# Graph attention on one core: a gather that leaves out the edges outside a slot's block of nodes

## The chip, the core and the metric

The kernel runs on one core of a Trainium2 chip. The metric is the device time of one execution in microseconds. The core has the engines TensorE (PE), VectorE (DVE), ScalarE (ACT) and GpSimd (POOL), the queue of SyncE (SP), which issues plain DMAs, and 16 DMA engines. Gathers by a list of indices are issued from GpSimd's queue.

## What is computed

One layer of graph attention with 12,500 nodes of 128 numbers, 200,000 edges with 64 numbers each, and 4 heads of 32. The edges come sorted by destination. The reference, cut to what matters (`_layernorm` and the first `maximum` make `h`):

```python
dst = jnp.minimum((12500 * jax.random.uniform(key, (200000,)) ** 2.0).astype(jnp.int32), 99999)
_o = jnp.argsort(dst, stable=True); src = src[_o]; dst = dst[_o]
...
h = jnp.maximum(_layernorm(x, axis=-1), 0.0)
h = (h @ W_node.T).reshape(num_nodes, H, HD)
e = (edge_features @ W_edge.T).reshape(num_edges, H, HD)
att = jnp.sum(jnp.concatenate([h[src], h[tgt], e], axis=-1) * a, axis=-1)
att = jnp.where(att > 0, att, 0.2 * att)
m = jnp.maximum(jax.ops.segment_max(att, tgt, num_segments=num_nodes), 0.0)
ex = jnp.exp(att - m[tgt])
denom = segment_sum(ex, tgt) + (num_edges - deg)[:, None] * jnp.exp(-m)
h_prime = segment_sum((ex / denom[tgt])[:, :, None] * h[src], tgt)
x = x + h_prime.reshape(num_nodes, H * HD)
```

## The kernel before

The nodes form 98 blocks of 128, the edges 1563 tiles of 128. A tile's edges can have destinations in more than one block. The kernel therefore works on slots: a slot is a tile together with one block, and a tile that reaches into a second block gets a second slot with the same 128 edges. There is room for 1664 slots (NS), in 52 groups (NG) of 32 (G), and each group has two halves of 16 (GS).

The program has four stages, each of which ends with all engines waiting for each other.

Stage 1 makes the tables of slots, nearly all of it on VectorE, in a chain in which each operation waits for the one ahead (`link`). With TensorE it selects for each slot the source indices `src_i` (one column of 128 a slot), the block `block_s`, and `rel_s`, the destination counted from the start of the slot's block: 0 to 127 for an edge inside the block, negative or 128 and more for one outside. The loop over `TB` = 13 column blocks (lines 295 to 306) copies these out; behind it come `block_1h` (line 308), the indices of the edge scores and the flags of chunks, which SyncE's queue stores to memory (line 193).

Stage 2 makes the table of nodes, `node_table`: for each node its 128 projected numbers and 4 scores, 528 bytes. GpSimd only sets `acc`, the sums of all nodes, to zero here (line 432).

Stage 3 is the loop over the groups. GpSimd gathers for each slot the 128 table rows of its source indices into `gath`, which holds two groups (line 661); once a group it gathers the edge scores too (line 650). After every 16 gathers it waits until they have landed (`PACE`). SyncE's queue loads the edges' numbers, TensorE and ScalarE make the edge scores from them. VectorE adds the scores (line 866, which needs the group's gathers), forms running maxima, multiplies the rows with the weights into `vals` (line 959) and adds each slot's sums to its block in `acc` (line 996), whose number is read at run time. Each slot has a one-hot matrix `onehot_b` (line 845: is `rel_s` equal to the column's number), whose rows for edges outside the block are all zero; TensorE multiplies it with `vals` (line 726), so the outside edges add zero times what stands in their rows.

Stage 4 divides the sums, adds `x` and stores the output.

The order on each engine is the order in which the code is written: GpSimd's queue in stage 3 is 32 gathers of line 661 a group, one of line 650 ahead of the 25th, and the two waits.

Of the kernel before, what the change touches and what calls it, by code (L numbers as in the profile page):

```python
# [14 lines left out]
P = 128  # L15
N_BLOCKS = -(-N_NODES // P)
N_TILES = -(-N_EDGES // P)
TB = -(-(N_TILES + N_BLOCKS - 1) // P)
NS = TB * P
G = 32  # L20
GS = G // 2
# [7 lines left out]
HC = HD + 1  # L29
ACC = HEADS * HC  # L30
PAD_DST = 1 << 20
NODE_GROUP = 7
N_NODE_GROUPS = N_BLOCKS // NODE_GROUP
EPS = 1e-5


def gat_kernel(nc, x, src, dst, ea, w_node, w_edge, a, out):
    f32, bf16, i32 = mybir.dt.float32, mybir.dt.bfloat16, mybir.dt.int32
    ALU = mybir.AluOpType
# [9 lines left out]
    with ctx:  # L49
        def sb(name, shape, dt):  # L50
            return ctx.enter_context(nc.sbuf_tensor(name, shape, dt))
# [19 lines left out]
        src_i = sb("src_i", [P, NS], i32)  # L71
        rel_s = sb("rel_s", [P, NS], bf16)
# [37 lines left out]
        def v3(t, cols):  # L110
            return t.rearrange("p (a c) -> p a c", c=cols)
# [3 lines left out]
        def tmp(n):  # L115
            off = [0]
            for m in (NS,) * 5 + (2 * P * TB,):
                off.append(off[-1] + m)
            return acc[:, off[n]:off[n + 1]]

        t_dst, t_a, t_b, t_c, t_last = tmp(0), tmp(1), tmp(2), tmp(3), tmp(4)
        sel = tmp(5).rearrange("p (k s) -> p k s", k=TB)
        gath_flat = gath[:, :, :, :].rearrange("p a s r -> p (a s r)")
# [10 lines left out]
        i_iota = of_flat[:, 0:2 * P].bitcast(i32)  # L134
        reset = src_i[:, :].bitcast(f32)
        tile_s, tile_here = t_b, t_c
        i_firstkey, key_t = oh_flat[:, 0:NS], oh_flat[:, NS:2 * NS]

        with ExitStack() as stage:
            def ssem(name):  # L140
                return stage.enter_context(nc.semaphore(name))
# [26 lines left out]
            def tiles(n):  # L168
                return dst[n:n + NS * P].rearrange("(k q p) -> q k p", q=P, p=P)

            with nc.Block() as block:  # L171
                @block.sync
                def _(sp):
                    sp.dma_start(v3(i_dst, P), tiles(1)).then_inc(s_ints, 16)
                    sp.dma_start(v3(i_src, P), src.rearrange("(k q p) -> q k p", q=P, p=P)).then_inc(s_ints, 16)
                    sp.dma_start(v3(i_other, P), tiles(0)).then_inc(s_prev, 16)
                    sp.dma_start(wn[:, :], w_node).then_inc(s_w, 16)
                    for j in range(2):
                        sp.dma_start(we2[:, j, :], w_edge).then_inc(s_w, 16)
                    sp.wait_ge(s_amat0, 1)  # L180
                    for h in range(HEADS):
                        sp.dma_start(a_mat[h * HD:(h + 1) * HD, h:3 * HEADS:HEADS],
                                     a[h, :].rearrange("(s d) -> d s", s=3),
                                     allow_slow_non_contiguous=True).then_inc(s_a, 16)
                    sp.wait_ge(s_prev_free, 1)
                    sp.dma_start(v3(i_other, P), tiles(2)).then_inc(s_next, 16)
                    sp.wait_ge(s_chunk, 1)
                    sp.dma_start(prev_keys[1:C, :, 0:1], chunk_keys[0:C - 1, 1, :, P - 1:P], allow_slow_non_contiguous=True).then_inc(s_prevkey, 16)
                    sp.dma_start(prev_keys[0:1, 1, 0:1], chunk_keys[C - 1:C, 1, 0, P - 1:P]).then_inc(s_prevkey, 16)
                    sp.wait_ge(s_flags, 1)  # L190
                    for b in range(2):
                        w = min(C, NG - b * C)
                        sp.dma_start(flags[b * C:b * C + w, :, :], chunk_flags[0:w, b, :, :]).then_inc(s_flags_out, 16)
                    sp.wait_ge(s_flags_out, 32)
# [21 lines left out]
                def _(dve):  # L216
                    step = [0]

                    def link(ins):

                        step[0] += 1
                        ins.then_inc(s_dve, 1)
                        dve.wait_ge(s_dve, step[0])

                    V = nc.vector
# [63 lines left out]
                    for k in range(TB):  # L289
                        link(V.tensor_scalar(vals[:, 0:2, 0:P], v3(iota[:, :], P), before[:, k:k + 1], None, ALU.is_ge))  # L290
                        V.scalar_tensor_tensor(out=sel[:, k, :].rearrange("p (c s) -> p c s", s=P), in0=v3(iota[:, :], P), scalar=end[:, k:k + 1],
                                               in1=vals[:, 0:2, 0:P], op0=ALU.is_lt, op1=ALU.mult).then_inc(s_sel, 1)
                        dve.wait_ge(s_sel, k + 1)

                    for k in range(TB):
# [7 lines left out]
                                               op0=ALU.mult, op1=ALU.add).then_inc(s_selfree, 1)  # L303
                        dve.wait_ge(s_selps, 2 * k + 2)
                        V.tensor_copy(i_firstkey[:, c], bank[3][:, 0:P])
                        V.tensor_copy(tile_s[:, c], bank[3][:, P:2 * P]).then_inc(s_selfree, 1)
                    dve.wait_ge(s_selfree, 2 * TB)
                    link(V.tensor_scalar(block_1h[:, :], block_s[:, :], pcol[:, 0:1], None, ALU.is_equal))
                    link(V.tensor_scalar(block_row[:, :], block_s[0:1, :], float(N_BLOCKS), None, ALU.min))
                    link(V.scalar_tensor_tensor(out=slot_no[:, :], in0=block_s[:, :], scalar=-float(P), in1=i_firstkey,  # L310
                                                op0=ALU.mult, op1=ALU.add))
# [85 lines left out]
        with ExitStack() as stage:  # L397
# [5 lines left out]

            W = NODE_GROUP
            WP = NODE_DIM + 2 * HEADS
# [12 lines left out]
            s_split, s_ttps, s_acc0 = ssem("tgt_split"), ssem("tgt_transposed"), ssem("acc_zeroed")  # L418
# [10 lines left out]
            with nc.Block() as block:  # L429
                @block.gpsimd  # L430
                def _(pool):
                    pool.memset(acc[:, :], 0.0).then_inc(s_acc0, 1)  # L432

                @block.sync
# [135 lines left out]
        with ExitStack() as stage:  # L570
# [7 lines left out]
            s_g = [ssem(f"rows_gathered{q}") for q in range(4)]  # L578
# [24 lines left out]
            def iterations(eng, start, body, finish):  # L603
                start(Group(0))
                for n in range(NG):
                    body(Group(n), n > 0, n + 1 < NG, n + 2 < NG)
                finish(Group(NG - 1))

            with nc.Block() as block:
# [34 lines left out]
                @block.gpsimd  # L644
                def _(pool):
                    def gather_edges(g):
                        for t in (min(g.n, NTG - 1), min(g.n, NTG - 1) - 1):
                            if t >= 0:
                                pool.wait_ge(s_er[t % 2], 16 * (t // 2 + 1))
                        nc.gpsimd.indirect_dma_start(  # L650
                            out=edge_t[:, g.r, :], out_offset=None, in_=edge_rows[0:min(g.n + 1, NTG) * P, :],
                            in_offset=bass.IndirectOffsetOnAxis(ap=edge_idx[:, g.n:g.n + 1], axis=0)).then_inc(s_et[g.r], 16)

                    def body(g, prev, nxt, second):
                        for a in range(2):
                            if g.n >= 2:
                                pool.wait_ge(s["vals"], g.n * 2 + a - 3)
                            for j in range(GS):
                                if a == 1 and j == GS // 2:
                                    gather_edges(g)  # L660
                                nc.gpsimd.indirect_dma_start(  # L661
                                    out=gath[:, g.r, a * GS + j, :], out_offset=None, in_=table,
                                    in_offset=bass.IndirectOffsetOnAxis(ap=src_i[:, g.n * G + a * GS + j:g.n * G + a * GS + j + 1], axis=0)).then_inc(s_g[2 * g.r + a], 16)
                                if j % PACE == PACE - 1:
                                    pool.wait_ge(s_g[2 * g.r + a], g.use * (16 * GS) + 16 * (j + 1))

                    iterations(pool, lambda g: None, body, lambda g: None)
# [165 lines left out]
                def _(dve):  # L833
# [131 lines left out]
                    def load_blocks(g, a):  # L965
                        blocks = []
                        for part in range(GS // 8):
                            _, b = nc.values_load_multi_w_load_instructions(
                                block_row[:, ds(g.n * G + a * GS + 8 * part, 8)], engines=[mybir.EngineType.DVE], min_val=0,
                                max_val=N_BLOCKS, skip_runtime_bounds_check_because="clamped to N_BLOCKS in stage 1")  # L970
                            blocks += b
                        return blocks
# [55 lines left out]
        with ExitStack() as stage:  # L1028
# [5 lines left out]

            W = 2 * NODE_GROUP
            n_out = N_BLOCKS // W
# [70 lines left out]
```

## Time and profile before

| | |
|---|---|
| time, median of 3 runs | 2682.41 us (2681.25 to 2682.56) |
| the profiled execution | 2685.02 us, its span 2682.7 us |
| busy share of the span | PE 45%, PEld 38%, DVE 64%, ACT 22%, POOL 61% |
| stage 1, 2, 3, 4 | 0 to 150.9, to 262, to near 2633, to 2682.7 us |
| memory | 183.85 MB read, 16.31 MB written, 75 GB/s over the span |
| granted TensorE clock, mean | 0.683 |

The span is the time from the first to the last instruction of the core; what the time has beyond it lies around the program. Busy is the time in which an engine executes; idle time ahead of an instruction is put down to what released it, and "issue" is idle time in which it waited for nothing that the profile shows. PEld is the weight load of TensorE. A lower-case q behind an engine's name is its sequencer, which issues DMAs and register operations. A line number such as L661 is a line of the kernel before.

### The profile page before, as it was taken

How to read it: one execution, taken by the hardware profiler on the slowest of the kernel's cores; microseconds unless marked ns; L12 is line 12 of the kernel's file. 1: busy time of each engine (PE TensorE's matmuls, PEld its weight loads, DVE VectorE, ACT ScalarE, POOL GpSimd, SP SyncE). 2: the span in 40 equal slices, each digit the busy share in tenths (PEclk: the TensorE clock that was granted, in tenths of full speed). 3: DMA queues.
4: the chain of work that ended last, by engine and by line, in shares of the span. 5: the costliest groups of instructions: out<-in, count | busy, mean ns of one | idle time of the engine just before them, and what ended most of it. 6: DMA issues, size and time to landing. Idle time of an engine off the chain costs nothing. (4 is left out here: it accounts for less than half of the span.)

```text
span 2682.7 us, 29095 instructions
## 1 busy us (share of the span) xinstructions
PE 1213.0 (45%) x8465; PEld 1013.4 (38%) x8465; DVE 1724.3 (64%) x4490; ACT 588.3 (22%) x1044; POOL 1648.1 (61%) x1729
## 2 busy tenths in 40 slices
PE   2635444535454545354545454545453545443431
PEld 1634233434343434343434343434343434343331
DVE  6588356565657565756566666666656666666666
ACT  0022212222222222222222222222222222221210
POOL 0010667667677766777777777776767767777740
PEclk9957666766666667676766676767666667665656
DMA  2034423232323232323232323232323232222226
GB/s 53 1 84 139 122 67 84 67 83 68 84 68 83 68 83 68 84 68 84 68 84 67 84 68 83 69 84 67 84 67 84 68 83 67 53 51 50 51 33 192
DMA packets 147213, 202.13 MB, mean 75 GB/s; under 512 B 55900, under 2 KB 113328, under 8 KB 140784
## 3 DMA queue, kind: packets, MB, share of 16 engines
q0 software_dynamic: 54912, 115.98, 18.9%
q1 hardware_dynamic: 79487, 77.88, 9.5%
q10 hardware_dynamic: 12656, 6.42, 0.8%
q8 instruction: 69, 1.13, 0.2%
q14 instruction: 89, 0.72, 0.1%
HBM read 183.85 MB, written 16.31 MB: 75 GB/s over the span
## 5 line engine op out<-in xcount | busy, mean ns | idle before, releaser
L661 POOL DMA_INDIRECT gath<-node_table,src_i x1664 | 1583.6, 952 | 778.8 <-issue 475.4
L726 PE MATMUL bank<-vals,onehot 128*128 128x132 f32 x3328 | 689.4, 387 | 892.3 <-DVE acc L996 517.9
L726 PEld LDWEIGHTS bank<-vals,onehot 128*128 128x128 f32 x3328 | 642.3, 290 | 912.6 <-issue 519.1
L996 DVE TENSOR_TENSOR acc<-acc,bank 128x132 f32 x1664 | 484.7, 291 | 354.9 <-PE bank L726 81.8
L780 ACT COPY onehot_t<-ps_oht 128x2048 bf16<-128x2048 bf16 x104 | 194.1, 1866 | 1014.6 <-PE ps_oht L696 1003.3
L789 ACT CAST onehot<-onehot_b 128x384 f32<-128x384 bf16 x624 | 279.1, 474 | 318.2 <-PE bank L726 311.6
L696 PE MATMUL ps_oht<-ident_b,onehot_b 128*128 128x128 bf16 x1664 | 163.7, 277 | 341.0 <-DVE onehot_b L845 341.0
L696 PEld LDWEIGHTS ps_oht<-ident_b,onehot_b 128*128 128x128 bf16 x1664 | 147.0, 129 | 348.4 <-DVE onehot_b L845 345.4
L866 DVE TENSOR_TENSOR zs<-gath,te 128x128 f32<-128x128 f32 x52 | 20.0, 385 | 397.6 <-DMA gath<-node_table,src_i 397.6
L845 DVE TENSOR_TENSOR onehot_b<-bank,rel_s 128x2048 bf16<-128x2048 f32 x104 | 237.1, 2282 | 0.0
L959 DVE TENSOR_TENSOR vals<-gath,bank 128x2048 f32<-128x2048 f32 x104 | 237.0, 2278 | 0.0
L688 PE MATMUL bank<-eattr,w_eatt 128*32 128x512 f32 x392 | 182.3, 609 | 5.2 <-DMA eattr<-edge_attr_in 4.5
L432 POOL MEMSET acc<- 128x13068 f32 x1 | 11.0, 10988 | 137.8 <-POOLq L171 137.8
L793 ACT ACTIVATE bank<-arg 128x128 f32<-128x128 f32 x52 | 14.6, 281 | 356.9 <-DVE arg L940 356.9
L688 PEld LDWEIGHTS bank<-eattr,w_eatt 128*32 128x32 f32 x392 | 39.9, 112 | 109.4 <-issue 105.1
L709 PEld LDWEIGHTS bank<-tgt_slot,onehot_t 128*128 128x128 bf16 x1664 | 55.9, 97 | 54.8 <-issue 38.6
L709 PE MATMUL bank<-tgt_slot,onehot_t 128*128 128x12 bf16 x1664 | 61.5, 183 | 13.7 <-ACT onehot_t L780 13.7
L914 DVE COPY ends_back<-chunk_out 4x64 f32<-4x64 f32 x208 | 57.3, 276 | 4.8
L650 POOL DMA_INDIRECT edge_t<-edge_scores,edge_idx x52 | 49.1, 944 | 15.8 <-issue 15.8
L892 DVE COPY chunk_max<-ends_t 4x64 f32<-4x64 f32 x208 | 52.4, 252 | 6.9 <-DVE ends_t L887 0.4
L772 ACT COPY edge_out<-bank 32x512 f32<-32x512 f32 x49 | 28.2, 575 | 98.0 <-PE bank L688 98.0
L982 DVE TENSOR_TENSOR acc<-acc,alpha 128x132 f32 x52 | 15.4, 297 | 51.6 <-issue 51.6
(182 smaller groups left out, 1135.7 us busy)
## 6 DMA issues: line engine op xcount, KB each, us to landing
eattr<-edge_attr_in SPq DMA_DIRECT2D x49, 1024.0 KB, 5.4
gath<-node_table,src_i POOLq DMA_INDIRECT x1664
node_table<-onehot_b SPq DMA_DIRECT2D x14, 462.0 KB, 3.9
gath<-x_in SPq DMA_DIRECT2D x14, 448.0 KB, 4.6
gath<-x_in SPq DMA_DIRECT2D x7, 896.0 KB, 7.0
out_dram<-onehot_b ACTq DMA_DIRECT2D x7, 896.0 KB, 8.0
edge_scores<-edge_out SPq DMA_DIRECT2D x49, 64.0 KB, 2.0
onehot_b<-dst_in SPq DMA_DIRECT2D x3, 832.0 KB, 5.2
```

Of the source, the lines that this page charges most:

```text
L661: nc.gpsimd.indirect_dma_start(out=gath[:, g.r, a * GS + j, :], out_offset=None, in_=table, in_offset=bass.IndirectOffsetOnAxis(ap=src_i[: ...
L688: last = T.matmul(ps_edge, w_eatt[:, c, :], eattr[:, t % 2, c, :], start=(c == 0), stop=(c == 3))
L696: last = T.transpose(ps_oht[:, j, :], onehot_b[:, g.r, a * GS + j, :], ident_b[:, :])
L709: last = T.matmul(ps_te[:, 3 * HEADS * slot:3 * HEADS * (slot + 1)], onehot_t[:, j, :], tgt_slot[:, :, slot], start=True, stop=True)
L726: last = T.matmul(SUM_BANK[b % 3][:, (j % 3) * ACC:(j % 3 + 1) * ACC], onehot[:, b % 3, j % 3, :], vals[:, j, :], start=True, stop=True)
L780: S.copy(onehot_t[:, :, :], ps_oht[:, :, :]).then_inc(s["oht"], 1)
L789: S.copy(onehot[:, b % 3, 0:w, :], onehot_b[:, g.r, a * GS + j:a * GS + j + w, :]).then_inc(s["cast"], 1)
L845: V.tensor_tensor(onehot_b[:, g.r, a * GS:(a + 1) * GS, :], ps_iota.unsqueeze(1).broadcast_to((P, GS, P)), rel_s[:, ds(g.n * G + a * GS, G ...
L892: V.tensor_copy(chunk_max[:, :].rearrange("p (e x) -> p e x", e=2)[:, :, q:q + 4 * C - 3:4], ends_t[q * C:q * C + HEADS, :].rearrange("p ( ...
L914: V.tensor_copy(ends_back[q * C:q * C + HEADS, :].rearrange("p (e c) -> p e c", e=2), chunk_out[:, :].rearrange("p (e x) -> p e x", e=2)[: ...
L959: V.tensor_tensor(vh[:, :, :, 0:HD], gath[:, g.r, a * GS:(a + 1) * GS, 0:NODE_DIM].rearrange("p s (h c) -> p s h c", h=HEADS), half_of(ps_ ...
L996: V.tensor_tensor(a_blk, a_blk, SUM_BANK[(j // 3) % 3][:, (j % 3) * ACC:(j % 3 + 1) * ACC], ALU.add).then_inc(s["added"], 1)
```

## The change

Stage 1 gets five operations on VectorE. They form 1 where `rel_s` lies outside 0 to 127 (not for empty slots) and 0 elsewhere, multiply it with 65,536 and add it to the source index. The gathers get a bound, the last row of the table, 12,543, and the instruction to leave out an index above it instead of reporting an error: nothing is written to that row of `gath`, and what stood there remains. So that a row that is left out never holds something undefined, GpSimd sets the last 128 columns of `gath`, which stage 1 doesn't write, to zero in stage 2. The gather of edge scores and all else stay as they are.

```diff
+OUTSIDE = 1 << 16
...
+        t_x, t_y = t_a, t_last
...
                     dve.wait_ge(s_selfree, 2 * TB)
+                    link(V.tensor_scalar(t_x, rel_s[:, :], 0.0, None, ALU.is_lt))
+                    link(V.scalar_tensor_tensor(out=t_y, in0=rel_s[:, :], scalar=-float(P * (N_BLOCKS + 1)), in1=t_x, op0=ALU.is_gt, op1=ALU.mult))
+                    link(V.scalar_tensor_tensor(out=t_x, in0=rel_s[:, :], scalar=float(P), in1=t_y, op0=ALU.is_ge, op1=ALU.add))
+                    link(V.tensor_copy(t_y, src_i[:, :]))
+                    link(V.scalar_tensor_tensor(out=src_i[:, :], in0=t_x, scalar=float(OUTSIDE), in1=t_y, op0=ALU.mult, op1=ALU.add))
                     link(V.tensor_scalar(block_1h[:, :], block_s[:, :], pcol[:, 0:1], None, ALU.is_equal))
...
+                    pool.memset(gath_flat[:, 5 * NS:], 0.0).then_inc(s_acc0, 1)
                     pool.memset(acc[:, :], 0.0).then_inc(s_acc0, 1)
...
                                 nc.gpsimd.indirect_dma_start(
                                     out=gath[:, g.r, a * GS + j, :], out_offset=None, in_=table,
-                                    in_offset=bass.IndirectOffsetOnAxis(ap=src_i[:, g.n * G + a * GS + j:g.n * G + a * GS + j + 1], axis=0)).then_inc(s_g[2 * g.r + a], 16)
+                                    in_offset=bass.IndirectOffsetOnAxis(ap=src_i[:, g.n * G + a * GS + j:g.n * G + a * GS + j + 1], axis=0),
+                                    bounds_check=N_BLOCKS * P - 1, oob_is_err=False).then_inc(s_g[2 * g.r + a], 16)
```

VectorE at the end of the selection in stage 1, before (bank is a PSUM bank, the others are names of the code; acc lends its memory to the tables here):

```order
L305 COPY onehot_b<-bank 128x128
L306 COPY acc<-bank 128x128
L308 TENSOR_SCALAR block_1h<-gath,pcol 128x1664
L309 TENSOR_SCALAR block_row<-gath 1x1664
L310 SCALAR_TENSOR_TENSOR gath<-gath,onehot_b 128x1664
```

and now:

```order
L307 COPY onehot_b<-bank 128x128
L308 COPY acc<-bank 128x128
L310 TENSOR_SCALAR acc<-rel_s 128x1664
L311 SCALAR_TENSOR_TENSOR acc<-rel_s,acc 128x1664
L312 SCALAR_TENSOR_TENSOR acc<-rel_s,acc 128x1664
L313 CAST acc<-src_i 128x1664
L314 SCALAR_TENSOR_TENSOR src_i<-acc 128x1664
L315 TENSOR_SCALAR block_1h<-gath,pcol 128x1664
```

Five operations over all slots stand ahead of the one that makes `block_1h`; the rest of the chain follows as it was.

GpSimd from stage 2 into the loop, before:

```order
L430 UNCONDITIONAL_BRANCH
L432 MEMSET acc 128x13068
L429 UNCONDITIONAL_BRANCH
L644 UNCONDITIONAL_BRANCH
L661 DMA gath<-node_table,src_i 128x132 x24
L650 DMA edge_t<-edge_scores,edge_idx 128x128
L661 DMA gath<-node_table,src_i 128x132 x32
```

and now:

```order
L437 UNCONDITIONAL_BRANCH
L439 MEMSET gath 128x128
L440 MEMSET acc 128x13068
L436 UNCONDITIONAL_BRANCH
L652 UNCONDITIONAL_BRANCH
L669 DMA gath<-node_table,src_i 128x132 x24
L658 DMA edge_t<-edge_scores,edge_idx 128x128
L669 DMA gath<-node_table,src_i 128x132 x32
```

One memset comes in, and the number and order of the gathers stay. Register operations are not among these rows: the program of the changed kernel has one register move ahead of each gather of line 669, which puts the bound, 12,543, into a register that the gather reads.

## Rows read from the trace of the kernel before

**Rows 1.** The page: span, busy us (share of the span) and instructions.

```profile
span 2682.7 us, 29095 instructions
...
PE 1213.0 (45%) x8465; PEld 1013.4 (38%) x8465; DVE 1724.3 (64%) x4490; ACT 588.3 (22%) x1044; POOL 1648.1 (61%) x1729
```

**Rows 2.** The waits: engine, line, releaser: us in total, times, longest.

```profile
POOL gath L661 <- issue: 475.4, 1560, 0.3
DVE zs L866 <- DMA gath<-node_table,src_i: 397.6, 52, 25.3
...
POOL gath L661 <- DMA gath<-node_table,src_i: 202.3, 103, 5.1
```

**Rows 3.** Groups of GpSimd: shapes, count, busy us, mean ns, idle before them.

```profile
L661 POOL DMA_INDIRECT gath<-node_table,src_i x1664 | 1583.6, 952 | 778.8 <-issue 475.4 <-DMA gath<-node_table,src_i 202.3 <-POOLq L429 101.1
L650 POOL DMA_INDIRECT edge_t<-edge_scores,edge_idx x52 | 49.1, 944 | 15.8 <-issue 15.8
L432 POOL MEMSET acc<- 128x13068 f32 x1 | 11.0, 10988 | 137.8 <-POOLq L171 137.8
```

**Rows 4.** Line 661: duration ns min/median/max, first and last start us.

```profile
L661 POOL DMA_INDIRECT gath<-node_table,src_i x1664: 938/945/1113, 263.0 to 2588.2; - x185
```

**Rows 5.** Timeline: start us, us, engine, line, operation, count, idle before.

```profile
1024.68 0.95 POOL L661 DMA_INDIRECT gath<-node_table,src_i  x1 [0.30 <-issue]
...
1027.42 0.39 DVE L866 TENSOR_TENSOR zs<-gath,te 128x128 f32<-128x128 f32 x1 [6.83 <-DMA gath<-node_table,src_i]
1027.56 1.01 POOL L661 DMA_INDIRECT gath<-node_table,src_i  x1 [1.92 <-DMA gath<-node_table,src_i]
```

**Rows 6.** DMA: the gathers' queue, packets, MB, share; issues to landing.

```profile
q0 software_dynamic: 54912, 115.98, 18.9%
...
edge_t<-edge_scores,edge_idx POOLq DMA_INDIRECT x52, 2.5
```

**Rows 7.** Timeline of GpSimd, start of the program and of stage 2.

```profile
0.24 0.10 POOL L1101 MEMSET const-float32-0.0<- 128x1 f32 x1 [0.24 <-issue]
0.27 0.10 POOL L1101 MEMSET const-float32-1.0<- 128x1 f32 x1
...
0.74 0.20 POOL L198 MEMSET ident<- 128x128 f32 x1 [0.29 <-POOLq L1101]
...
150.93 10.99 POOL L432 MEMSET acc<- 128x13068 f32 x1 [137.84 <-POOLq L171]
```

**Rows 8.** Line 996 (count: min/median/max ns) and the timeline around it.

```profile
L996 DVE TENSOR_TENSOR acc<-acc,bank x1664: 291/291/294, 328.6 to 2632.9; 128x132 f32 x185
L996 DVEq FUSED_REGOPS  x1612: 57/57/57, 329.0 to 2632.8; - x180
...
1027.84 0.33 DVE L869 STREAM_TRANSPOSE bank<-zs 128x128 f32<-128x128 f32 x1
1028.20 0.29 DVE L872 TENSOR_TENSOR z<-bank,edge_t 128x128 f32<-128x128 f32 x1
...
1037.55 6.79 DVE L996 TENSOR_TENSOR acc<-acc,bank 128x132 f32 x16 [0.97 <-issue]
```

**Rows 9.** Timeline: VectorE and the flags' stores at the end of stage 1.

```profile
125.91 0.29 DVE L298 CAST src_i<-bank 128x128 int32<-128x128 f32 x1 [1.81 <-PE bank L390]
...
127.23 0.28 DVE L306 COPY acc<-bank 128x128 f32<-128x128 f32 x1
127.55 1.08 DVE L308 TENSOR_SCALAR block_1h<-gath,pcol 128x1664 bf16<-128x1664 f32 x1
...
129.72 1.89 DVE L310 SCALAR_TENSOR_TENSOR gath<-gath,onehot_b 128x1664 f32<-128x1664 f32 x1
...
148.31 0.41 DVE L350 TENSOR_TENSOR onehot<-onehot,onehot_t 32x256 f32<-32x256 f32 x1
...
148.75 0.74 SPq L193 DMA_DIRECT2D chunk_flags<-onehot  x2
```

**Rows 10.** Timeline of VectorE early in stage 1: a cast from integer.

```profile
14.52 1.03 DVE L244 CAST acc<-onehot_b 128x1664 f32<-128x1664 int32 x1
```

## The prediction

> **What bounds the kernel now.** I read the busy line of the page first. No engine is above 64% of the span [rows 1], so the share says nothing, and the question is who waits for whom. In the list of waits VectorE waits for the gathers 52 times, once in each of the 52 groups of 32 slots, 397.6 us in all, 7.6 us a group; GpSimd waits for no computing engine in the loop, only for its own gathers to land, and otherwise stands 0.30 us between one gather and the next [rows 2]. The groups of GpSimd then close the account of the whole loop. 1664 gathers of 952 ns are 1583.6 us, the gaps between them 475.4 us, the 103 waits for landing 202.3 us, and the 52 gathers of edge scores 49.1 us with 15.8 us of gaps [rows 3]: 2326.2 us. The first gather starts at 263.0 us and the last at 2588.2 us [rows 4], and 2588.2 + 0.94 - 263.0 is 2326.1 us. So the middle of the span is one queue of gathers on GpSimd, with 263.0 us of preparation ahead of it and 2682.7 - 2589.1 = 93.6 us behind it. A group takes 33 x 1.25 us and two waits of near 2 us, 44.7 us. The timeline of one such wait shows what stands in it: the sixteenth gather of a half ends at 1025.63, its rows land, VectorE goes on at 1027.42 and GpSimd at 1027.56 [rows 5]. Any nanosecond that a gather gains or loses counts 1664 times; anything that moves only bytes counts nothing, for the gathers' queue keeps the DMA engines busy for 18.9% of the span [rows 6].
>
> **The change, part by part.**
> *How many rows are left out.* The destinations are sorted, a tile is 128 edges, and a tile whose edges reach into a second block of 128 nodes gets a slot for each. From the inputs as the reference draws them: 1658 slots are used of 1664, they hold all 200,000 edges once, and 12,224 rows of the 212,992 lie outside their slot's block, in 191 slots, none in most of the early groups and 256 to 512 in each of the last 30. That is 5.7% of the rows. The number of gathers stays 1664, and so do the two waits of a group.
>
> *Less data.* 12,224 rows of 528 bytes are 6.5 MB of 116 MB. The data is waited for only behind the sixteenth gather of a half, 103 times; of these gathers 16 leave rows out. The landing of a whole edge gather takes 2.5 us [rows 6] and the wait as a whole about 1.8 us after the end of the instruction. Were half of each such wait saved, it would be 16 x 0.9 = 14 us; I take nothing, since gathers of full size stand right ahead of these in the same engines.
>
> *Less generation, if the 0.94 us go by rows.* No gather of before leaves anything out, so both bounds are worked out. If a skipped row costs nothing and the whole 0.945 us [rows 4] goes by rows, a row is 7.4 ns and 12,224 rows are 90 us gained. If its index has still to be read, compared and stepped over, nothing is gained. The nearest rows are the gathers of table rows (528 bytes, 0.945 us) and of edge scores (512 bytes, 0.944 us) [rows 3]: neither size nor the table moves the duration, which leaves the number of indices, and that is 128 in every gather before and after. I take 0 and keep -90 us for the range. Beside it stand two statements of the Trainium skill that pull apart. "Perfetto Trace Analysis", section "DMA Instruction - SWDGE (GPSIMD)", says that the profiled end of such an instruction is the moment when the last of the two processors has generated its descriptors, not when the data has moved; the trace agrees, since the wait for the data begins only after the 0.94 us. By that, leaving descriptors out should shorten the instruction, up to the 90 us above. "DMA: Bandwidth & Descriptors", section "Anatomy of one DMA", holds generation to be small and variable, and most of a DMA's fixed time, some 2 us, to be the receipt of the write; no run here splits the 0.945 us.
>
> *The comparison itself.* Every gather now has a bound to compare 128 indices with, on the engine that is the bound. No row shows it. From below it is 0, if a comparison is made or hidden in the loop anyway. From above, the nearest row for a step on this engine is the memset of 13,068 elements a partition in 10.99 us [rows 7], 0.84 ns a step; one such step for each of 128 indices, one after the other, is 0.108 us a gather and 179 us in all, two are 358 us. I take 0: 7.4 ns a row leave room for a comparison beside the stores. This is the weakest term, and it is a rival below.
>
> *A register for the bound.* The order of instructions shows no new row, but the program has one register move ahead of each of the 1664 gathers, and where a gather used to wait for landing the wait now stands on the move. VectorE shows what this costs when it can't be prepared ahead: its adds read a block number through register operations of 57 ns, and 16 adds of 291 ns take 6.79 us, so (6.79 - 16 x 0.291) / 15 = 0.14 us between two, while two linked operations without registers stand 0.03 us apart (0.33 us from 1027.84, the next at 1028.20) [rows 8]. The difference is 0.11 us. At the 103 waits I charge it: 11 us. At the other gathers the move should be made while the gather ahead still runs, as GpSimd's queue takes work ahead: its first four memsets start 0.03 us apart and last 0.10 us each [rows 7]. Cover gone, it is at least 0.057 x 1664 = 95 us (the rival below).
>
> *Five operations on VectorE in the preparation.* They stand between the last copy out of the selection and the comparison for block_1h, in a chain where each waits for the one ahead; VectorE is busy from 125.91 to 148.72 us with no wait for another engine, the flags are stored right behind, and the second stage starts at 150.93 us [rows 7, 9]. So all of it is on the path. A comparison of one tensor with a number over 128x1664 takes 1.08 us, a scalar-tensor-tensor 1.89 us, a cast from integer 1.03 us [rows 9, 10]. One, three and one of these with five gaps of 0.04 us are 1.08 + 5.67 + 1.03 + 0.20 = 8.0 us. If the bf16 operand costs the first one the long form, it is 8.8; if it shortens the others to 1.08, it is 6.4.
>
> *The memset of the last 128 columns of gath.* 128x128 took 0.205 us on GpSimd [rows 7]; it stands ahead of the memset of acc in a stage in which GpSimd is idle for 101 us until the gathers start [rows 3]. Nothing, unless that idle time were gone, and then 0.2 us.
>
> **The sum.** 2682.7 + 8.0 + 11 + 0 + 0 = 2701.7 us of span. The profiled execution took 2685.0 us and the median of the runs is 2682.4, 0.3 us below the span itself; I take the span's sum less 0.3 us and round: **2701 us**. Nothing takes up the added time: VectorE's 7.6 us of waiting a group just moves, and behind the last gather the same 93.6 us follow.
>
> **The rivals.**
> *Skipped rows shorten the gather (faster).* For it speaks that the 0.945 us is the making of 128 entries; against it that every index is still read. At the full 7.4 ns a row it gives 2701 - 90 = 2611, at half of it 2656. It must gain 24 us, 27% of the 90, to be faster by more than 0.2%. VectorE would follow: at most 512 x 7.4 ns = 3.8 us a group against its 7.6 us.
> *The comparison costs a step for each index (slower).* Its place is the 0.945 us of each gather, its price 0.108 us x 1664 = 179 us for one step: 2880 us, for two 3059. It decides as soon as it is over 3 ns a gather, for GpSimd has no idle time to hide it in. For it speaks that GpSimd makes these entries by program; against it that 7.4 ns a row is roomy.
> *The register move isn't hidden.* The gap between gathers grows from 0.30 us by 0.057 to 0.11 us: 95 to 183 us, less the part charged already: 2785 to 2873 us. For it: the gap of 0.30 us is the same to 10 ns everywhere, as it would be if each gather were handed over only when the last had ended. Against it: the memsets.
> *The change doesn't do what it says* (all rows are still fetched, or their fetch is turned into something as dear): then only the costs remain, which is the forecast itself.
>
> **How the numbers follow.** Forecast, 2690 to 2715: 0.35. Gain by skipping: 0.27, of which 0.20 ends below 2677 (faster by over 0.2%, about what a measurement of this kernel can tell from no change) and 0.07 within it. Comparison by index: 0.26, of which 0.09 lies above 3000. Register move not hidden: 0.12. So faster 0.20, same 0.08, slower 0.72. The range reaches down to 2640, which takes in a gain of two thirds of the 90 us and leaves out about 0.06, and up to 3000, which leaves out about 0.09.
>
> **What the profile after would show.** The mean of the gather group: 952 ns if the forecast holds, near 1060 if the comparison costs a step; a spread of durations with a lower end well under 938 ns if skipping shortens, for 191 of 1664 only. The gaps ahead of gathers: 475 us for 1560, or 570 and more with the move in the open. The waits for landing: 202 us growing to some 213. The first gather near 271 us instead of 263. Packets or bytes of the gathers' queue 5.7% lower, if the rows are really left out. I would be wrong most of all if the whole population of gathers, also those that leave nothing out, changed its duration.

## The result: 140 us slower

The changed kernel takes 2824.6 us (2822.6 to 2825.7), the kernel before, run beside it, 2682.5 us. The ratio is 1.0527, with a 95% interval of 1.0509 to 1.0546. The span of the profiled execution grew from 2682.7 to 2822.5 us. The forecast was 2701 us: the direction was right, the size was not, by a factor of seven, and the rival of a comparison in each gather, at 2880 us, came nearer.

The page of the changed kernel, its span, its busy line and the gathers' queue (packets, MB, share of the DMA engines):

```profile
span 2822.5 us, 30765 instructions
...
PE 1212.9 (43%) x8465; PEld 1011.5 (36%) x8465; DVE 1708.6 (61%) x4495; ACT 587.9 (21%) x1044; POOL 1736.8 (62%) x1730
...
q0 software_dynamic: 54912, 109.57, 17.0%
```

Against [rows 1, 6] the queue moves 6.41 MB less, 5.5%: the 12,224 rows really are left out. The packets are as many as before, 54,912, and 12,224 rows of 528 bytes would be 6.45 MB; what is missing fits 4 bytes that still move for each row left out (12,224 x 524 is 6.41 MB). GpSimd is busy 89 us longer. Its groups in the changed kernel (busy us, mean ns, idle time ahead), and below them line 669 with minimum, median and maximum in ns and its first and last start:

```profile
L669 POOL DMA_INDIRECT gath<-node_table,src_i x1664 | 1671.5, 1004 | 820.6 <-issue 477.9 <-DMA gath<-node_table,src_i 241.1 <-POOLq L436 101.6
L658 POOL DMA_INDIRECT edge_t<-edge_scores,edge_idx x52 | 49.7, 956 | 15.8 <-issue 15.8
...
L669 POOLq MOVE  x1664: 29/29/29, 271.0 to 2713.7; - x185
L669 POOL DMA_INDIRECT gath<-node_table,src_i x1664: 991/997/1339, 271.8 to 2726.9; - x185
```

These answer to [rows 3, 4], and they hold the whole difference:

| term | before | after | difference, us |
|---|---|---|---|
| first gather starts | 263.0 | 271.8 | 8.8 |
| 1664 gathers, busy | 1583.6 | 1671.5 | 87.9 |
| gaps ahead of them ("issue") | 475.4 | 477.9 | 2.5 |
| waits for landing | 202.3 | 241.1 | 38.8 |
| gathers of edge scores, with gaps | 64.9 | 65.5 | 0.6 |
| behind the last gather | 93.6 | 94.6 | 1.0 |
| sum | 2682.8 | 2822.4 | 139.6 |

The 2.5 us of gaps are no gaps. The changed kernel has 102 waits for landing by this view where it had 103 before, and one more gap; the missing wait is the one below, 2.55 us long at the first gather of a half, and the view puts it down to "issue". With it the 103 waits are 243.7 us, 41.3 us more than before. A wait or two is misplaced like this in other runs too.

```profile
POOL gath L669 <- issue: 477.9, 1561, 2.5
...
1548.73 1.00 POOL L669 DMA_INDIRECT gath<-node_table,src_i  x1 [2.55 <-issue]
```

The least duration went from 938 to 991 ns [rows 4]: the whole population of gathers is longer, also the more than 1400 that leave nothing out. VectorE is busy no longer than before; it waits longer for the gathers, 553.5 us in all against 397.6 [rows 2]. Its line and GpSimd's waits for landing:

```profile
DVE zs L875 <- DMA gath<-node_table,src_i: 553.5, 52, 24.7
...
POOL gath L669 <- DMA gath<-node_table,src_i: 241.1, 102, 2.8
```

A wait of the changed kernel in the timeline, at the same place as [rows 5]; the idle time ahead is 2.43 us where it was 1.92, and the next gather follows 0.30 us behind, as ever:

```profile
1024.90 1.00 POOL L669 DMA_INDIRECT gath<-node_table,src_i  x1 [0.30 <-issue]
1028.33 0.99 POOL L669 DMA_INDIRECT gath<-node_table,src_i  x1 [2.43 <-DMA gath<-node_table,src_i]
1029.63 0.99 POOL L669 DMA_INDIRECT gath<-node_table,src_i  x1 [0.30 <-issue]
```

And the five operations on VectorE in stage 1, with the one that follows them:

```profile
127.79 1.03 DVE L310 TENSOR_SCALAR acc<-rel_s 128x1664 f32<-128x1664 bf16 x1
128.85 1.89 DVE L311 SCALAR_TENSOR_TENSOR acc<-rel_s,acc 128x1664 f32<-128x1664 bf16 x1
130.78 1.89 DVE L312 SCALAR_TENSOR_TENSOR acc<-rel_s,acc 128x1664 f32<-128x1664 bf16 x1
132.71 1.03 DVE L313 CAST acc<-src_i 128x1664 f32<-128x1664 int32 x1
133.77 1.89 DVE L314 SCALAR_TENSOR_TENSOR src_i<-acc 128x1664 int32<-128x1664 f32 x1
135.70 1.09 DVE L315 TENSOR_SCALAR block_1h<-gath,pcol 128x1664 bf16<-128x1664 f32 x1
```

From 127.79 to 135.70 they take 7.9 us. GpSimd leaves stage 1 at 159.1 us where it was 150.9, 8.2 us later. The rest of the 8.8 us at the first gather is within the scatter of stage 2: in the kernels that share this stage 1 the first gather starts anywhere from 267.5 to 272.9 us, and at 269.1 and 272.9 in two profiles of one and the same kernel.

### The profile page after: what moved, and what is told of

The parts are those of the page before. It is cut to its first block and busy times, and to the rows that moved or that the text cites. A ratio compares the mean times of both kernels' runs of the same rounds, so it can differ in the third digit from the quotient of the medians.

```text
span 2822.5 us, 30765 instructions
## 1 busy us (share of the span) xinstructions
PE 1212.9 (43%) x8465; PEld 1011.5 (36%) x8465; DVE 1708.6 (61%) x4495; ACT 587.9 (21%) x1044; POOL 1736.8 (62%) x1730
## 3 DMA queue, kind: packets, MB, share of 16 engines
q0 software_dynamic: 54912, 109.57, 17.0%
## 5 line engine op out<-in xcount | busy, mean ns | idle before, releaser
L669 POOL DMA_INDIRECT gath<-node_table,src_i x1664 | 1671.5, 1004 | 820.6 <-issue 477.9
L735 PEld LDWEIGHTS bank<-vals,onehot 128*128 128x128 f32 x3328 | 635.3, 287 | 1045.1 <-issue 646.6
L875 DVE TENSOR_TENSOR zs<-gath,te 128x128 f32<-128x128 f32 x52 | 19.7, 379 | 553.5 <-DMA gath<-node_table,src_i 553.5
L901 DVE COPY chunk_max<-ends_t 4x64 f32<-4x64 f32 x208 | 44.6, 214 | 6.7
L559 PE MATMUL bank<-w_proj,gath 128*128 128x136 f32 x196 | 40.6, 384 | 14.9 <-ACT gath L543 14.9
```

The lines of the kernel that those rows point to most:

```text
L669: nc.gpsimd.indirect_dma_start(out=gath[:, g.r, a * GS + j, :], out_offset=None, in_=table, in_offset=bass.IndirectOffsetOnAxis(ap=src_i[: ...
L735: last = T.matmul(SUM_BANK[b % 3][:, (j % 3) * ACC:(j % 3 + 1) * ACC], onehot[:, b % 3, j % 3, :], vals[:, j, :], start=True, stop=True)
L901: V.tensor_copy(chunk_max[:, :].rearrange("p (e x) -> p e x", e=2)[:, :, q:q + 4 * C - 3:4], ends_t[q * C:q * C + HEADS, :].rearrange("p ( ...
```

## Experiments

All expectations below go by one theory, called Theory A (A1 to A3 are its parts): the gathers are longer because they carry a bound, whatever it does to the rows, and the waits are longer because they now stand on a register move. The rivals are in the expectations. Where an edit is shown, `...` stands for what is left out of it.

**The preparation alone.**

```diff
-link(V.scalar_tensor_tensor(out=src_i[:, :], in0=t_x, ...))
+link(V.scalar_tensor_tensor(out=t_dst[:, :].bitcast(i32), in0=t_x, ...))
...
-    ..., axis=0), bounds_check=N_BLOCKS * P - 1, oob_is_err=False).then_inc(...)
+    ..., axis=0)).then_inc(...)
```

> The preparation alone: the five operations of stage 1 and the small memset stay, but the marks are written to a scratch table instead of the source indices, and the gathers have no bound. So nothing is left out and nothing is checked. Theory A (the bound itself lengthens each gather by 52 ns and each landing wait by 0.4 us, the preparation costs only its own chain): 2682.5 + 8 to 9 = 2691 us, ratio 1.003; the gathers stay at 0.945 us, the waits for landing at 202 us. Rival B (something of the preparation, such as the source table written a second time, slows the gathers): 2780 us or more, gathers near 1.00 us.

Measured: 2690.2 us, ratio 1.0036 (1.0022 to 1.0051). Its gathers are those of before, and they start 8.8 us late:

```profile
L669 POOL DMA_INDIRECT gath<-node_table,src_i x1664: 938/944/1112, 271.8 to 2593.3; - x185
```

So the preparation costs its own chain and nothing that can be seen beside it; rival B falls.

**The bound alone, no row outside it.** Only the first edit of the run above; the bound stays.

> The changed kernel, but the marks go to a scratch table: every index is inside the bound, all 212,992 rows are fetched, and the gathers still carry the bound with the instruction to skip. Theory A (the cost is in carrying a bound, the rows left out change nothing): 2824 us, ratio 1.053, gathers 0.997 us, the same as with rows left out. Rival C (skipping rows is what costs, or what saves): gathers back near 0.945 us and 2705 us if skipping costs; 2850 to 2900 us if the 12,224 rows left out had been saving something like the 90 us worked out before.

Measured: 2823.8 us, ratio 1.0539 (1.0522 to 1.0557), the same as the changed kernel's within the intervals, with all 115.98 MB moved:

```profile
L669 POOL DMA_INDIRECT gath<-node_table,src_i x1664: 991/997/1347, 271.2 to 2724.9; - x185
```

Leaving 5.7% of the rows out is worth nothing that can be measured, and carrying the bound costs all of the 52 ns. What in the instruction takes them, the comparison or the reading of the bound, no run separates.

**A bound that reports instead of skipping.** `oob_is_err=True` in the same kernel.

> As the run before, all indices inside the bound, but an index above it would be reported as an error instead of being skipped. Theory A1 (any comparison with a bound costs the 52 ns): 2824 us, gathers 0.997 us. Rival D (only the mode that skips costs it, since then the write side too must know which rows fall out): gathers near 0.945 us, 2705 to 2745 us, the upper end if the longer landing waits stay.

Measured: 2843.0 us, ratio 1.0606 (1.0588 to 1.0623); median of a gather 1013 ns:

```profile
L669 POOL DMA_INDIRECT gath<-node_table,src_i x1664: 1007/1013/1333, 270.2 to 2750.9; - x185
```

Rival D falls: it is not the skipping. Reporting costs 16 ns a gather more by the medians (13 by the means), which Theory A1, with its 2824 us, had not foreseen either.

**One register for the bound.**

```diff
+last_row = pool.to_reg(N_BLOCKS * P - 1)
...
-bounds_check=N_BLOCKS * P - 1, oob_is_err=False
+bounds_check=last_row, oob_is_err=False
```

> The changed kernel with the bound put into one register ahead of the loop, instead of one register move ahead of each gather; rows are left out as in the changed kernel, and the waits for landing stand on the gathers again. Theory A2 (the register moves are hidden between gathers, 29 ns each, and only those behind a wait count; the longer waits come from the wait standing on the move): the gathers stay at 0.997 us, the waits for landing fall from 241 us to near 202 us, 2824 - 39 = 2785 us, ratio 1.038. Rival E (the waits are longer because gathers with a bound land later): no change, 2824 us. Rival F (the moves also lengthen the gathers): gathers at 0.945 us and some 2700 us.

Measured: 2768.4 us, ratio 1.0330 (1.0313 to 1.0347). The gathers keep their 997 ns. All 103 waits are seen again, and they fall to 192.4 us, from 243.7 with the one that was put down to issue:

```profile
L671 POOL DMA_INDIRECT gath<-node_table,src_i x1664: 991/997/1179, 267.9 to 2670.6; - x185
...
POOL gath L671 <- DMA gath<-node_table,src_i: 192.4, 103, 3.3
```

So 51 of the 140 us go with the moves, 0.50 us a wait. The time fell by 56; 3.9 us of that are an earlier first gather, 267.9 us, which the scatter of stage 2 covers. Rivals E and F fall. Theory A2 expected the waits back at 202 us and 2785 us; they are 10 us shorter than in the kernel before, and why is open.

**All rows left out.** `src_i` becomes `src_i + 65536` everywhere.

> The changed kernel with 65,536 added to every source index, so that every one of the 212,992 rows is left out and the gathers move nothing: this leaves the whole gather of source rows out of the computation. It asks what a skipped row is worth. Theory A (the instruction reads and handles 128 indices in 0.997 us whether a row is made or not): gathers at 0.997 us, the landing waits shorter by at most the movement of 67 KB, near 0.5 us each, 2780 to 2824 us. Rival G (a skipped row saves its share of the time): at 7.4 ns a row the gathers would fall to near 0.1 us and TensorE and VectorE would set the time, 2300 us or less; at a quarter of it, 0.75 us, 2400 us.

Measured: 2774.1 us. The first line is the gathers' queue (3.41 of its 4.37 MB are edge scores, 0.85 MB are 4 bytes for each of the 212,992 rows, and the last 0.11 MB stand beside the rows in the kernel before too), the second their duration, the third the waits:

```profile
q0 software_dynamic: 54912, 4.37, 1.9%
...
L669 POOL DMA_INDIRECT gath<-node_table,src_i x1664: 991/997/1342, 271.3 to 2680.7; - x185
...
POOL gath L669 <- DMA gath<-node_table,src_i: 193.6, 102, 3.6
```

A skipped row takes as much of GpSimd's time as a fetched one, and the queue still has its 54,912 packets. It looks as if each skipped index still gets an entry, of 4 bytes instead of 528, which would be why skipping saves no time; that is read from the bytes and not tested. With no row fetched at all the waits fall by 47 us, 0.46 us each: that is what the rows add to the wait for landing, and the most that leaving rows out could have saved here.

**Fewer indices instead of skipped ones, without and with the bound.** `gath[0:64, ...]` and `src_i[0:64, ...]` in the gather, in the kernel with the preparation alone and in the changed one.

> Without a bound, with the preparation of the changed kernel, each gather of source rows takes only its first 64 indices and partitions; the other half of each slot's rows is left out of the computation. It asks how the 0.945 us divide. Theory A expects a part by index and a fixed part, without a number from before; half the duration (0.47 us) if all of it goes by rows, 0.945 us if none. With 0.47 us GpSimd would need 33 x 0.77 + 4 = 29 us a group and the engines that compute some 37 us, 2300 us in all; with 0.7 us 2300 to 2330 us.

> The same 64 indices a gather, now with the bound and the marks of the changed kernel. Theory A3 (the bound costs a comparison for each index): the gathers are longer than in the run with 64 rows and no bound by half of 52 ns, 26 ns. Rival H (the bound costs a fixed amount for each instruction, such as handing the register over): longer by 52 ns with 64 rows as with 128.

Measured: 2617.8 and 2714.4 us. In this order, the gathers of the two runs:

```profile
L669 POOL DMA_INDIRECT gath<-node_table,src_i x1664: 899/908/1125, 270.5 to 2521.9; - x185
```

```profile
L669 POOL DMA_INDIRECT gath<-node_table,src_i x1664: 938/947/1193, 270.6 to 2618.8; - x185
```

Without a bound 64 indices take 908 and 128 take 945 ns: 0.58 ns an index, and by a line through the two, an estimate, 0.87 us that don't depend on the number. With the bound it is 947 and 997: 0.78 ns an index. So the bound costs 39 ns at 64 and 52 at 128, by a line through the two some 26 ns fixed and 0.2 ns an index. That lies midway between A3 (26 ns) and H (52 ns): each had half of it. The time of the first run, 2618 us, is also far from the 2300 us that it was expected to have if the duration went by rows. A run with the bound and the first 32 indices was meant to test the line:

> Gathers with the bound that take only the first 32 indices and partitions; three quarters of each slot's rows are left out of the computation. 128 indices took 0.997 us and 64 took 0.947 us. If the duration is a straight line in the number of indices (0.78 ns each above 0.897 us), it is 0.922 us here. If it goes in steps (for example by how many indices are handled at once, or by processor), it is at 0.947 us or near 0.90 us.

```profile
L669 POOL DMA_INDIRECT gath<-node_table,src_i x1664: 906/916/1082, 271.2 to 3611.9; - x185
```

916 ns instead of 922: not a perfect line (31 ns for the last 32 indices, 50 for the 64 ahead of them), but no step either, and the two parts of the bound's 52 ns are only as good as the line. Its time, 3730.3 us in a single run, says nothing, as told next.

**The moves and the waits in the whole kernel: runs that could not tell.** Three kernels were run twice: the one with one register and a move put back behind each wait, and the changed kernel and the one with one register, both with the wait moved behind the fourth gather of the next half.

> The kernel with one register for the bound, with a register move put back ahead of the first gather of each half only, which is where the wait for landing then stands: 104 moves instead of 1664 or 1. Theory A (what the moves cost is the wait standing on a move, 0.4 to 0.5 us at each of 103 waits, and moves elsewhere are hidden): the landing waits are back at about 241 us and the time near 2768 + 49 = 2817 to 2824 us, ratio 1.053. Rival J (each of the 1664 moves makes something later, for example in the reading of the program, and the wait only shows it): near 2768 to 2775 us, waits near 192 us.

> The changed kernel, moves and bound as they are, with the wait for the landing of a half moved behind the fourth gather of the next half, as in the same edit of the kernel before (2513 us). Theory A (bound 88 us over all gathers, preparation 9 us, moves free when nothing is waited for): 2513 + 88 + 9 = 2610 us, ratio 0.973. Rival K (a wait on a register move costs 0.4 us even when it is already fulfilled, since the queue can't be filled past it): 2610 + 42 = 2652 us.

> As the run before with one register for the bound and no moves in the loop. Theory A: 2606 to 2610 us, the same as with the moves. Rival K: 2606 to 2610 us here, but 2652 us with the moves.

Measured: 3530.3, 3590.3 and 3497.0 us, against 3613.4 us for the kernel before in the same set (3509.9, 3591.2, 3495.4 and 3603.6 in the second). The kernel before itself had taken near 2681 us in the sets ahead of these, so the 900 us are not of the edits. TensorE, ScalarE and VectorE waited long here where the profile shows no cause on this core (it writes "remote"), GpSimd's gathers were as long as ever, and GpSimd waited for VectorE instead of for its rows, in the third kernel:

```profile
DVE acc L1008 <- remote: 998.7, 109, 13.8
...
POOL gath L671 <- DVE vals L975: 901.5, 100, 21.4
```

GpSimd's queue is not the bound in these runs, so their times don't decide the question, and I took the other engines out of the loop. One difference stays unexplained: with the wait moved, the kernel with its 1664 moves took 93 and 96 us more than the one with one register, in both sets, where Theory A expected none and rival K 42 us. So the whole kernel with bound and moved wait was never measured with its queue as the bound.

**GpSimd's queue alone.** In the loop only the 1664 gathers with marks and bound and the waits for landing stay.

> Only GpSimd works in the loop over the groups: the 1664 gathers with marks and bound and their 104 waits for landing; the gathers of edge scores, the waits for VectorE and all work of TensorE, ScalarE, VectorE and SyncE in the loop are left out, so the output isn't the reference's. One register for the bound. From the run with one register: 1670 us of gathers, 475 us of gaps, 192 us of waits, with 270 us ahead and some 52 us behind: 2659 us.

> The same, with a register move ahead of the first gather of each half, on which the wait for landing stands. Theory A (a wait on a register move costs 0.4 to 0.5 us, moves elsewhere nothing): 192 + 49 = 241 us of waits, 2708 us. Rival J (each of the 1664 moves makes something later): within 5 us of the run with one register.

> The same loop with a register move ahead of every gather, as in the changed kernel, and the wait for a half behind the fourth gather of the next half, where it is fulfilled. Theory A (nothing is paid where the wait is fulfilled): 1670 us of gathers and 1663 gaps of 0.304 us, 2176 us, with 270 and 52 us around them 2498 us. Rival K (a wait on a move costs 0.4 us even when fulfilled): 2540 us, seen as 103 gaps of 0.7 us.

Measured: 2651.8, 2728.4 and 2497.4 us, against 2659, 2708 and 2498 expected. The waits with one register:

```profile
POOL gath L666 <- issue: 475.3, 1560, 0.3
POOL gath L666 <- DMA gath<-node_table,src_i: 188.7, 103, 2.0
```

with 104 moves behind the waits:

```profile
POOL gath L666 <- issue: 500.5, 1561, 2.6
POOL gath L666 <- DMA gath<-node_table,src_i: 238.5, 102, 2.5
```

with a move ahead of every gather and the waits fulfilled when they are reached:

```profile
POOL gath L664 <- issue: 490.1, 1609, 0.3
...
POOL gath L664 <- DMA gath<-node_table,src_i: 16.5, 54, 0.3
```

In GpSimd's queue alone Theory A stands: 104 moves behind waits bring back 50 us of waiting, 1664 moves with fulfilled waits cost nothing (no gap above 0.3 us), and rivals J and K fall. The second run has more that nobody expected: 25 us of idle time put down to issue. One gap of 2.63 us among it is the 103rd wait, so the moves cost 52.4 us of waiting, 0.51 us a wait; the other 23 us are 20 gaps of 1.44 us instead of 0.30, behind every fifth wait from the eighth, one gather on:

```profile
1007.40 0.99 POOL L666 DMA_INDIRECT gath<-node_table,src_i  x1 [2.32 <-DMA gath<-node_table,src_i]
1009.84 0.99 POOL L666 DMA_INDIRECT gath<-node_table,src_i  x1 [1.44 <-issue]
1011.13 1.00 POOL L666 DMA_INDIRECT gath<-node_table,src_i  x1 [0.30 <-issue]
```

What they are is open; the changed kernel, with its 1664 moves, has none of them.

**The waits for landing moved.** The kernel before, with the wait for a half's landing behind the fourth gather of the next half:

```diff
-if j % PACE == PACE - 1:
-    pool.wait_ge(s_g[2 * g.r + a], g.use * (16 * GS) + 16 * (j + 1))
+if j == 3 and 2 * g.n + a:
+    p, b = (g, 0) if a else (g + -1, 1)
+    pool.wait_ge(s_g[2 * p.r + b], (p.use + 1) * (16 * GS))
```

> The kernel before, with the wait for the landing of a half moved behind the fourth gather of the next half, where the half has long landed, so GpSimd never stands still for it. It asks whether GpSimd's queue really is the whole bound, so that each nanosecond taken off it comes out of the time. Theory A: 2682 - 200 = 2482 us, ratio 0.926, with VectorE's wait for the gathers down by about the same 200 us. Rival I (some other engine or the landing of rows takes over at once, or gathers following closer land later): 2600 to 2680 us.

Measured: 2513.2 us, ratio 0.9375 (0.9359 to 0.9390).

```profile
POOL gath L661 <- issue: 506.8, 1663, 0.3
...
DVE zs L867 <- DMA gath<-node_table,src_i: 239.9, 52, 20.8
```

All 103 waits of 202.3 us are gone, and each has left a plain gap of 0.30 us, 31.4 us in all: 171 us, and the span fell by 170.5. The expectation, 2482 us, had forgotten those gaps. Time taken off GpSimd's queue comes out of the whole, so this queue is the bound, and here the saving lies in the waits and not in the rows.

## Why the forecast had the size wrong

- *What bounds the kernel.* Right. The account of GpSimd's queue closes before and after, and what came onto it came out in the time.
- *Less data: nothing.* Right; with the bound alone and no row left out the time is the same.
- *Less generation: 0 taken, up to 90 us kept.* The value was right, the 90 us far off. I divided the whole 0.945 us by 128 rows to get 7.4 ns; the runs with 64 rows show 0.58 ns an index, and a skipped index saves none of that. The Trainium skill's page "Perfetto Trace Analysis", section "DMA Instruction - SWDGE (GPSIMD)", has the profiled instruction end with the last descriptor, which I read as support for the rival of a shorter gather; the gathers that fetch nothing take the same 997 ns, so the duration doesn't go by the rows fetched. The Trainium skill's page "DMA: Bandwidth & Descriptors", section "Anatomy of one DMA", calls generation small and variable: the part by index is small here, 74 of 945 ns at 0.58 ns each, but the fixed part of the instruction is 0.87 us.
- *The comparison: 0 taken.* This is the step that failed: a term put at nothing that measured 88 us, 53 ns a gather by the means, of the 121 us missing. The prediction had named this sign itself, a whole population of gathers that changes its duration. "7.4 ns a row leave room for a comparison" rested on the same false division. The rival put it at 108 ns for one step an index; it is about half of that, and part of it is fixed.
- *A register for the bound: 11 us.* Half right. The moves between gathers are hidden, as the memsets suggested. Behind a wait a move was taken at VectorE's price of 0.11 us; it is 0.40 us against the kernel before and 0.50 us against one register, 41 and 51 us. The rival of moves that aren't hidden had 2785 to 2873 us, which holds the measured time, but by luck: it put 95 to 183 us into the gaps between gathers, and those stayed at 0.30 us. The nearest row was of another engine.
- *Five operations: 8.0 us.* Measured 7.9, and 8.8 us at the first gather with the scatter of stage 2. *The memset:* 0.2 us, in a stage in which GpSimd still stood idle for 101.6 us, as forecast.
- *Nothing takes up the added time.* Right: behind the last gather 94.6 us against 93.6.

With the two terms as measured, 88 for 0 and 41 for 11, the forecast's own sum is 2701 + 88 + 30 = 2819 us, against 2824.6.

## What to carry to other kernels

When one queue is the bound, an edit that adds anything to each of its instructions needs a measured price before it is made: 53 ns times 1664 was 88 us, more than all the rest of the change cost (52 us) and more than leaving out every row would have saved (47 us). Don't divide a duration by its rows unless rows of two sizes stand in the profile. Look first at what the bounding queue waits for: two waits a group were worth 170 us. And a constant that an instruction reads belongs in a register ahead of the loop where a wait would otherwise stand on its move; that alone was 51 us here.

## What the runs showed of the hardware that I had not expected

- A gather of 128 rows from GpSimd's queue takes 945 ns without a bound, 997 with one that skips, 1013 with one that reports; with 64 rows 908 and 947, with 32 rows and the bound 916. It takes 997 ns when no row is fetched at all, and then 4 bytes a row are still counted in the queue, in as many packets.
- A wait that stands on a register move instead of on the gather itself makes the gather start 0.5 us later (103 waits of 188.7 us against 241.1 in the queue alone, 192.4 against 243.7 in the whole kernel, each second figure with the wait put down to issue). A register move of 29 ns between two gathers costs nothing, and in the queue alone none behind a fulfilled wait either.
- The rows of the gathers, 67 KB each, add 0.46 us to each wait for landing (241.1 us against 193.6 with no row fetched, 102 waits by either view).
